# Due times of the first batches' norms, projections and row maxima shifted by a table

## The reference

```python
x = x + attention(layernorm(x))      # 16 heads of 16, rotary embedding, causal softmax, Wo
x = x + moe(layernorm(x))            # softmax router over 16 experts in 4 groups; top 2 groups, top 4 experts
                                     # each expert: (silu(x W1) * (x W3)) W2, width 176
                                     # plus a shared expert of width 352 for every token
```

## Time and profile before

| | |
|---|---|
| runs | 865.42, 866.97, 2531.93 us; median 866.97 |
| profiled execution | 866.86 us, span 865.0 us |
| busy, share of the span | PE 752.6 us (87%), DVE 701.8 (81%), POOL 513.7 (59%), ACT 491.4 (57%) |
| granted TensorE clock, mean | 0.951 |
| TensorE busy, 40 slices of 21.6 us, in tenths | 3568999999999999999999859999999999999600 |
| granted clock in these slices | 9669999999999999999999899999999999999955 |

### The profile page before, as it was taken

How to read it: one execution, slowest core, us unless ns; L and a number is a source line. 1 busy time by engine, 2 the same in 40 slices (tenths; PEclk the granted TensorE clock), 3 DMA queues, 4 the chain that set the end, 5 groups by cost and what they waited for, 6 DMA issues and landing times.

```text
span 865.0 us, 21098 instructions
## 1 busy us (share of the span) xinstructions
PE 752.6 (87%) x6109; PEld 680.9 (79%) x6109; DVE 701.8 (81%) x2394; ACT 491.4 (57%) x1284; POOL 513.7 (59%) x489
## 2 busy tenths in 40 slices
PE   3568999999999999999999859999999999999600
PEld 3556788888888888888887648899999999999600
DVE  4556788999999999999988698798988988888425
ACT  4335555565656565656555455677777777666400
POOL 4223433665666565756665566777787888778700
PEclk9669999999999999999999899999999999999955
DMA  3566644875568556754661377999999888877699
GB/s 121 140 176 185 183 138 124 224 239 154 187 207 246 158 197 200 240 177 165 167 188 55 97 250 231 214 200 200 192 200 191 143 142 137 143 135 108 77 397 376
DMA packets 115744, 157.92 MB, mean 183 GB/s; under 512 B 13488, under 2 KB 100016, under 8 KB 115632
## 3 DMA queue, kind: packets, MB, share of 16 engines
q1 hardware_dynamic: 88032, 115.52, 45.9%
q0 software_dynamic: 26736, 36.85, 23.9%
q10 hardware_dynamic: 864, 4.19, 1.2%
HBM read 74.55 MB, written 81.43 MB: 180 GB/s over the span
## 4 chain that ended last, share of the span: by engine, by line
PE 51%; DVE 21%; DMA 8%; issue 8%; POOL 6%; SPq 3%; ACT 2%; POOLq 0%; DVEq 0%; ACTq 0%
PE bank L707 25%; PE bank L965 9%; DVE row_max L1305 6%; PE bank L938 3%; PE bank L747 3%; DMA acc<-acc_scr 3%; PE bank L791 2%; DVE rope_b L1291 2%; PE bank L714 2%; DVE stats L1257 2%; PE bank L953 2%; POOL roped L1686 2%; PE bank L954 2%; PE bank L751 2%; POOL roped L1684 1%
## 5 line engine op out<-in xcount | busy, mean ns | idle before, releaser
L1719 POOL DMA_INDIRECT acc_scr<-yb,tokens x143 | 225.1, 1574 | 57.3 <-issue 25.1
L1708 POOL DMA_INDIRECT rows_scr<-xn,rows_of x128 | 126.2, 986 | 59.0 <-issue 31.9
L707 PE MATMUL bank<-wexp,xbT_hi 128*128 (+1 forms) x572 | 149.7, 343 | 0.0
L1305 DVE TENSOR_REDUCE row_max<-bank 128x2 f32<-128x512 f32 (+1 forms) x192 | 127.3, 679 | 15.3 <-PE bank L751 15.0
L1071 ACT ACTIVATE probs<-bank 128x512 f32<-128x512 f32 x192 | 108.7, 604 | 25.9 <-PE bank L791 25.1
L965 PE MATMUL bank<-wexp,upT 112*128 (+3 forms) x572 | 120.2, 303 | 0.6 <-ACT yb L1183 0.6
L747 PE MATMUL bank<-kst,qst 112*128 112x256 f32 (+1 forms) x512 | 97.8, 297 | 19.1 <-DMA kst<-qk_scr 17.3
L1693 POOL TENSOR_SCALAR_AFFINE_SELECT probs<-probs 128x1024 f32<-128x1024 f32 x64 | 70.9, 1108 | 62.5 <-ACT probs L1071 62.3
L747 PEld LDWEIGHTS bank<-kst,qst 112*128 112x128 f32 x512 | 79.9, 199 | 31.4 <-DMA kst<-qk_scr 18.8
L707 PEld LDWEIGHTS bank<-wexp,xbT_hi 128*128 128x128 f32 x572 | 92.8, 189 | 0.0
L707 PE MATMUL bank<-wexp,xbT_lo 128*128 (+1 forms) x286 | 92.3, 323 | 0.0
(11 more groups left out here) (227 smaller groups left out, 2212.6 us busy)
## 6 DMA issues: line engine op xcount, KB each, us to landing
xb<-rows_scr SPq DMA_DIRECT2D x143, 138.0 KB
qk_scr<-ropeds_hi SPq DMA_DIRECT2D x64, 256.0 KB, 2.4
qst<-qk_scr SPq DMA_DIRECT2D x64, 192.0 KB, 3.6
kst<-qk_scr SPq DMA_DIRECT2D x64, 192.0 KB, 3.7
acc<-acc_scr SPq DMA_DIRECT2D x12, 768.0 KB, 15.1
qk_scr<-ropeds_lo SPq DMA_DIRECT2D x32, 256.0 KB, 2.6
acc_scr<-zero SPq DMA_DIRECT2D x10, 768.0 KB
st<-in_wexp SPq DMA_DIRECT2D x36, 152.0 KB
```

What stands on the lines that cost most here:

```text
L707: ins = e.matmul(region, stationary(s, k), moving(m, k), start=(j == 0), stop=(j == n - 1), skip_group_check=True)
L1305: e.tensor_reduce(row_max[:, half, h:h + n, i], view, AX.X, ALU.max).then_inc(s_max)
L1708: e.indirect_dma_start(rows_scr[:, :], bass.IndirectOffsetOnAxis(ap=rows_of[b % 2][:, i, r:r + 1].bitcast(U32), axis=0), x2[:, i, :], None ...
L1719: e.indirect_dma_start(acc_scr[j % NACC][:, :], bass.IndirectOffsetOnAxis(ap=tokens[j % NTOK][:].bitcast(U32), axis=0), yb[j % NYB][:], No ...
```

## The change

A table of shifts, in batches, is added to the start times of some stages. Nothing else differs.

```diff
--- before.py
+++ after.py
@@ -90,6 +90,7 @@
 
 
 SOONER = {"route": [-0.14, -0.28, -0.42], "shared": [0, 0.25, 0.32]}
+FIRST_SOONER = {("attend", 0): -0.05, ("maxima", 0): -0.1, ("maxima", 1): -0.2, ("maxima", 2): -0.05, ("norm", 1): -0.45, ("norm", 2): -0.4, ("norm", 3): -0.3, ("project", 1): -0.45, ("project", 2): -0.4, ("project", 3): -0.2}
 TAKES = {
     "project": {7: ["xT"], 10: ["q0"], 12: ["q1"], 15: ["v"]},
     "maxima": {**{k: [f"m{k}"] for k in range(UNITS)}, 7: ["mT0"],
@@ -119,7 +120,7 @@
 def plan():
 
 
-    runs = [[b + start + (SOONER[stage][b - B + 3] if stage in SOONER and b >= B - 3 else 0), (end - start) / steps, stage, b, n]
+    runs = [[b + start + (SOONER[stage][b - B + 3] if stage in SOONER and b >= B - 3 else 0) + FIRST_SOONER.get((stage, b), 0), (end - start) / steps, stage, b, n]
             for b in range(B) for stage, ((start, end), steps, n) in STAGES.items() if stage != "load" or b >= 2]
     runs += [[B - 1 + 5.28, 0.880 / 8, "tables", B - 1, 8], [0, 0.6 / 10, "load_wqkv", 0, 7], [0.1, 3.4 / 19, "setup", 0, 19],
              [B - 1 + 2.35, 1.67 / EXPERT_STEPS, "experts", 0, EXPERT_STEPS],
```

## The result

| | before | changed |
|---|---|---|
| median | 867.33 us | 861.97 us |
| runs (6 each) | 865.42 to 2531.93 | 860.79 to 864.40 |
| ratio, 95% interval | | 0.9944 [0.9927, 0.9961] |
| profiled execution | 866.86 us, span 865.0 | 864.4 us, span 862.6 |

The changed kernel is 5.4 us faster by the medians (the first three runs of before had the median 866.97 us; one of its six took 2531.93 us, which the median hardly feels). The interval of the ratio allows a gain of 3.4 to 6.3 us. The forecast was 11.6 us of gain: the direction is right, the size more than twice too large. The profiled execution of after is the slowest of its six, so the shift is read from the steps in the first 100 us and not from its end.

What follows compares the result with a forecast made beforehand. The first 100 us bound the gain: the pipe fills one batch at a time, while regular batches keep TensorE full. A gain of 11.6 us, chosen between bounds of 7.6 and 15.8, gave 866.9 - 11.6 = 855.3 us; range 850 to 863 us.

Steps and rivals of the forecast that it cites:

- position 285: Step order differs only in its first 285 of 2,474 positions; how much earlier this point is reached stands to the end.
- The start at 27.3 us: Batch 1's projection products start at 27.3 us, in TensorE's idle stretch, at the lower clock.
- The second stall for `kst`: TensorE's 3.76 us idle for batch 1's stack, ending at 54.56 us before; forecast gone, stack ready at about 47 us.
- SyncE's queue: Place of the slower rival (0.04): batch 0's maxima rows follow batch 1's whole stack; landed at 46.6 us, needed at 53.
- Batch 0's maxima, to 47.2 us: VectorE's rope chain, 11 row maxima, moments and two turns end at 47.2 us, 3.3 us sooner.
- Batch 1's maxima and attention 0, to 67.2 us: VectorE's 14.5 us of work and 5.5 us of estimated waits end at 67.2 us, 9.5 us sooner.
- TensorE's limit: Work to batch 2's last maxima copy: at most 21.8 us gain; 12.5 at packing 0.988, 7.6 at some 0.875.
- When attention 0 begins, about 53 us: Start of attention 0's products, at about 53 us, with 38.1 us of TensorE work left from there.
- VectorE's bound (88.3 us): Batch 2's maxima on VectorE: 19.5 us with 1.6 us of waits, ending at 88.3 us, 15.8 us sooner.
- the gaps stay and the clock stays low: Rival, chance 0.17: 37 to 65 us at the lower clock leaves 3 to 6 us of gain, 861 to 864 us.
- Everything packs: Rival, chance 0.07: position 285 before 86.8 us, 17.3 us sooner, waits in the two middle steps absent; 842 to 849.5 us.
- The rule weighed: Wsg's low part, with two SBUF inputs, blocks GpSimd; batch 0's second-half values up to 1.65 us late, sum 857 us.

Runs made afterwards that it cites:

- e4: Changed kernel's table cut to the entries for batch 1's norm and projection and batch 0's maxima, rest ordered as before; ratio to before 0.9955.
- e12: e1 plus eight more idle matmuls ahead of attention 0's sixth product; ratio to before 0.9897, batch 2's last maxima copy at 94.32 us.
- e5: Changed kernel run again unaltered beside the experiments, on other chips than the first; ratio to before 0.9925, batch 2's last maxima copy at 97.80 us.
- e7: Kernel before, order untouched, with 50, 8 and 16 idle matmuls ahead of three steps; ratio to before 0.9934, batch 2's last maxima copy at 98.18 us.
- e1: Changed kernel with 33 idle matmuls where TensorE waits for row maxima and xT; ratio to before 0.9906, batch 2's last maxima copy at 95.66 us.
- e3: Changed kernel with Wsg's split moved right behind batch 2's xT; ratio to before 0.9934, batch 2's last maxima copy at 97.34 us.
- e8: Changed kernel with e2's and e3's edits, GpSimd's early clearing of V buffers and 47 idle matmuls; ratio to before 0.9883.
- e9: e8 with Wsg loaded behind batch 1's stacks, its high part ahead of batch 2's high Q, its low part as in the changed kernel; ratio to before 0.9863.
- e2: Changed kernel with the second query and key buffers cleared behind batch 0's xT; ratio to before 0.9903, batch 2's last maxima copy at 94.58 us.

## Why the forecast was right and wrong

**What held.** The bound was read rightly: the start is a chain with holes, the rest runs at its own pace, and the shift at position 285 is the gain (5.7 us there, 5.4 us by the medians). The start at 27.3 us came at 27.49. The second stall for `kst` is gone. That batch 1's projection belongs in the idle stretch is the effect (e4). SyncE's queue was no danger: batch 0's second maxima rows were issued at 49.84 us, when they existed, with batch 1's stacks all issued by 43.5 us.

**The steps that failed** are "Batch 0's maxima, to 47.2 us" and "Batch 1's maxima and attention 0, to 67.2 us", both sized with full-clock durations, and with them the term that TensorE's limit starts from, "When attention 0 begins, about 53 us".

| step | forecast | changed | clock held up (e12) |
|---|---|---|---|
| batch 0's maxima done | 47.2 | 49.8 | 48.4 |
| attention 0 begins | 53 | 57.9 | 53.8 |
| batch 1's maxima done | 67.2 | 74.4 | 70.6 |
| batch 2's maxima done (104.1 - 11.6) | 92.5 | 98.4 | 94.6 |

The last column is the test: with the clock held up (1.00 from 34 us on), attention 0 begins within 0.8 us of where the forecast had it, and 3.8 of the missing 5.9 us come back (3.5 against e5). Of the 4.9 us at attention 0 the rows name four pieces, 4.0 us together, as much as e12 gives back there (57.89 to 53.84): 1.3 us at batch 2's Q (2.73 instead of 1.44), 0.4 us at its turn (1.06 us against 0.60 for the same four matmuls in e12), some 1 us at the two units behind it (eight matmuls in 2.15 us against 1.19 in e7), and 1.3 us at the second half of batch 0's maxima (6.32 us between the first two copies, 5.02 in e1), where VectorE had to wait for its units.

The rest is in VectorE's small terms. At batch 1's last copy e12 is still 3.4 us behind the forecast. 1.2 us of it stand before batch 0's copy: batch 1's low K is done at 37.9 us instead of 37.3, and each of the two turns of the maxima takes 1.0 to 1.1 us instead of 0.8. The other 2.2 us are in the next step, 22.2 us instead of 20.0. This is e12's stretch of it:

```profile
48.39:70.62 22.23, 20.88 (x179) 15.19 (x177) 16.28 (x29) 12.82 (x25) 8.36 (x9) 1.00 0.58 172
```

VectorE works 16.3 us there where I had 14.5: Wsg's low part took 2.13 us instead of 1.6, the moments 1.8 instead of 1.1, and the two rope low parts 0.85 and 0.77 instead of 0.6. It waits 5.9 us where I had 5.5; the wait for the maxima copy, behind ScalarE's Wsg part and three exponentials, was 1.5 of my 2.0. e3, which moves the split away, gives back 0.5 us.

**TensorE's limit** held as a pair of bounds, and its start was the wrong input. In the changed kernel, from attention 0's first product to batch 2's last copy:

```profile
57.89:98.38 40.49, 36.36 (x335) 28.85 (x337) 32.64 (x70) 25.94 (x52) 15.89 (x17) 1.00 0.64 178
```

That is 36.4 us of work at a packing of 0.898 (0.941 by the forecast's 38.1 us), between the bounds of 0.988 and 0.875. I had chosen 0.965 (38.1 of 39.5 us), and this choice is the smaller part of the error: 1.0 of the 5.9 us, against 4.9 at the start. From batch 1's last copy on, every kernel with the shifts of batches 2 and 3 takes 24.0 us, so the earlier delay wasn't made up there. VectorE's bound (88.3 us) never came to bear.

**The rivals.** The first one happened: "the gaps stay and the clock stays low", with its place (37 to 65 us; it was 42.5 to 56), the 3 to 6 us of gain that it leaves (5.4) and its times of 861 to 864 us (861.97). It had 0.17. The measured time lies in the stated range only because the range took in most of this rival. Its evidence was in the earlier trace rows, 0.50 granted at 50 to 60 us with 62% busy, and I discounted it by the row of 60 to 80 us at 1.00, which has a different neighbourhood. The forecast's own terms had VectorE freeing a bank every 0.6 us or later from 37 to 47 us, against units of 0.36 to 0.63 us; that this leaves TensorE waiting before the first turn (3.56 us) I didn't work out. The mechanism also had a size: 11.2 us at the lower level hold 5.6 us of excess, of which 3.5 to 3.8 us came out at the end. That is about two thirds, where I had assumed half. *Everything packs* reached down to 842 us, 3 us below what the forecast's own limit of 21.8 us allows (845.1).

The rule weighed (the Trainium skill, SBUF — State Buffer, the shared port pair) would have moved the sum by 1.7 us and was left inside the bounds. The trace has the effect: 2.08 us for batch 2's first rope add beside Wsg's low part, and 0.73 us in the changed kernel, where the low part stands elsewhere. But the low part itself now takes 2.13 us instead of 1.65, beside GpSimd's causal select. So some half us now falls on VectorE. The rule on bursts that each start cold (the Trainium skill, TensorE: Matmul & The Clock Gate, on oscillation) was the better guide here. The changed kernel agrees with it behind its wait of 3.56 us (0.50), and e1 behind its wait of 2.03 us (0.55). But a wait doesn't settle it: behind 2.24 us at 64.36 us the changed kernel stayed at 1.00, and so did e8 behind 3.06 us.

## What to carry to other kernels

A busy share read at a granted clock of 0.50 is worth half: in a stretch where engines take turns, price TensorE's pieces at both levels, and take the level from a measured stretch that has the same short pieces and waits as the new plan, not from a neighbouring one. A few matmuls on constants into an unused bank, put into the waits, need no reordering and can tell in one run what the clock is worth, if the granted clock of that run shows that they held it (in e9 they did not). In a pipe that fills, move the work that only clears or splits things into another engine's wait first; here it was worth 3.2 us at the last copy (e2), beside 5.7 us for the change of order.

## What the runs showed of the hardware

- Idle matmuls in an unchanged order made the program 0.66% faster (e7), about as much as the whole change of order (0.56 and 0.75%).
- The clock fell behind a TensorE wait of 2.03 us (e1, 0.55 from 61 to 64.7 us), and stayed at 1.00 with eight more matmuls in that wait (e12). It fell behind waits of 2.04 us (e2, 0.63) and 2.61 us (e9, 0.55), and did not fall behind 2.24 us (changed kernel) and 3.06 us (e8). The length of the one wait does not decide it in these runs.
- The same subtraction on VectorE with 128x1440 elements took 1.65 us in e7 and 2.13 us in after. In e7 GpSimd's rope add beside it took 2.08 us instead of 0.74; in after it ran beside a causal select, which took the 1.09 us that it takes elsewhere. GpSimd's timeline of e7, then of the changed kernel:

```profile
59.27 2.08 POOL L1694 TENSOR_TENSOR roped<-rope_a,rope_b 128x256 f32<-128x256 f32 x1 [1.10 <-DVE rope_b L1301]
```

```profile
65.57 1.09 POOL L1694 TENSOR_SCALAR_AFFINE_SELECT probs<-probs 128x1024 f32<-128x1024 f32 x1 [3.18 <-ACT probs L1072]
```
